# LoRA A read in place from 32 small transfers on two queues, in a conditional-LoRA and mixture-of-experts kernel

## The chip, the cores and the metric

One core of one Trainium2 chip runs the program. The metric is device time in microseconds (us) of one execution, as the median of several runs. The profiled execution is one run more, taken by the hardware profiler, with times counted from its first instruction.

## The reference

x is 32 sequences of 32 tokens of 512 numbers. Each sequence picks one of 32 adapters. The first part is a dense layer with that sequence's low-rank addition (rank 16, scaled by 2); its result feeds a router over 16 experts in 4 groups, of which each token takes two, and a shared feed-forward part.

```python
base_out = jnp.einsum('bti,oi->bto', x, W) + b
A = lora_As[adapter_mapping]              # (32, 512, 16)
Bm = lora_Bs[adapter_mapping]             # (32, 16, 512)
lora_h = jnp.einsum('bti,bir->btr', x, A)
xt = base_out + jnp.einsum('btr,bro->bto', lora_h, Bm) * SCALING
logits = xt @ router_w + router_b         # softmax, bias, two groups of four, two experts
h = silu(xt @ w1 + b1) * (xt @ w2 + b2)   # for each expert, weighted by its gate; the same once, shared
out = x + sum_e gate_e * (h_e @ w3 + b3) + shared
```

## The kernel before

The 1024 tokens are worked in two halves of 512 (`n` = 0, 1), the 512 dimensions in 4 chunks of 128 (`KC`, `k` or `m`). Products that need precision are made of three (`product`, L990): each operand is split into a rounded part (`_h`, a cast by ScalarE) and a remainder (`_l`, whole minus rounded, a subtraction by VectorE in `rest`, L680).

Every engine runs a program written out by hand, in order, and semaphores join them; a wait therefore holds everything that is written behind it on the same engine. The order around the change is this.

TensorE (from L1101) makes 10 warm-up products, then the dense layer of the first half chunk by chunk (`cond_first`), of the second half block by block (`cond_second`), and between them the LoRA work in 4 groups of 8 sequences (`g`): `turn_lora` turns the group's gathered A through PSUM bank 6, `lora_h` multiplies x by it, `cond_lora(n)` adds the low-rank part of a half. `logits_turned` and `logits` are the router, `shared_up` the shared part. Much later come `dense_up`, the two most used experts (from L1161), and the gathered rest.

GpSimd (L372) makes constants, then gathers rows of `lora` (a row is 512 numbers of A and 512 of B) by index, a group of 128 rows a transfer (`gather_lora`, L392); the last two wait for the buffer of the first two. The indices come from VectorE (L675 to L678).

SyncE (L316) only issues transfers: x's first half, six small ones, then, behind a wait for that half, the second half; behind the gather of group 1 the shared weights (`sw12`) and two more; then the stores of x's turned rows `xt_rows` for each half (L339, behind `xt_ready`), x again (L345), the two dense experts' weights (L354), and so on, all in one queue.

ScalarE (L456) issues the dense layer's weights, casts, copies A back from PSUM (`copy_loraA`), and issues the 4 MB of zeros for `y_rows` (L527), behind a wait for the last gather. Its later casts `hi_w12e` (L564) are those of the dense experts' weights. VectorE (L654) makes the remainders, masks the LoRA product (`mask_lh`), turns x's rows (`turn_xt`), chooses the experts (`choose`) and subtracts for the dense experts (`lo_w12e`).

Of the kernel before, what the change touches and what calls it, by code (L numbers as in the profile page):

```python
# [14 lines left out]
P = 128  # L15
# [6 lines left out]
SEQ_PER_GROUP = P // RANK  # L22
COLS, QUARTER = 32, P // 32
# [28 lines left out]
def program(nc, x, xT, seq_slot, condWT, cond_b, lora, router_w, router_b, router_bias,  # L52
# [5 lines left out]
    with ExitStack() as ctx:  # L58
# [30 lines left out]
        def at(kib, name, shape, dt=F32):  # L89
# [13 lines left out]
        zeros = at(16, "zeros", [P, DIM])  # L103
# [29 lines left out]
        lora_raw = at(152, "lora_raw", [P, 2, 2 * DIM])  # L133
        loraA_sb = at(160, "loraA_sb", [P, KC, P])
        lhT_split = at(162, "lhT_h", [P, 2, GT], F32R), at(164, "lhT_l", [P, 2, GT], F32R)
# [25 lines left out]

        slot_i = sb("slot_i", [P, GROUPS_L], I32)
# [50 lines left out]
        seq_in, small_in, x_in, sw3_in = (  # L213
            sem("seq_in"), sem("small_in"), sem("x_in"), sem("sw3_in"))
# [6 lines left out]
        w3_in = [sem(f"w3_in{s}") for s in range(STATIC)]  # L221
        lora_in = [sem(f"lora_in{g}") for g in range(GROUPS_L)]

        condW_hi, condW_done = sem("condW_hi"), sem("condW_done")
        xT_hi, xT_done, sw12_hi, sw12_done = sem("xT_hi"), sem("xT_done"), sem("sw12_hi"), sem("sw12_done")
        loraA_copied, xt_whole, loraB_hi, loraB_done = (
            sem("loraA_copied"), sem("xt_whole"), sem("loraB_hi"), sem("loraB_done"))
        zeros_ready = sem("zeros_ready")
# [3 lines left out]
        loraA_turned, lh_done, lh_masked = sem("loraA_turned"), sem("lh_done"), sem("lh_masked")  # L232
# [35 lines left out]
        def cond_bank(n, m):  # L268
            return bank[(4, 0, 1, 2)[m] if n else m]
# [5 lines left out]
        def unit_bank(u, m):  # L275
            return bank[((3, 6), (4, 0), (1, 2), (3, 7), (4, 0), (1, 2), (6, 1), (4, 0))[u][m]]
# [8 lines left out]
        def gate_bank(s):  # L285
            return bank[(4, 0)[s % 2]]
# [4 lines left out]
        def sum_bank(i):  # L291
            return bank[(2, 7, 6, 1, 4, 0, 3, 5)[i]]

        def turned_bank(b):
            return bank[(6, 1)[b % 2]]

        def y_bank(b):
            return bank[(2, 7)[b % 2]]
# [18 lines left out]
        def _(sp):  # L317
            def load_xT(n, k):
                sp.dma_start(xT_raw[n][:, k, :], xT[n, k]).then_inc(xT_in[n * KC + k], 16)  # L319

            load_xT(0, 0)
            sp.dma_start(slot_i[:], seq_slot).then_inc(seq_in, 16)
            for k in range(1, KC):
                load_xT(0, k)
            sp.dma_start(condb_sb[:], cond_b).then_inc(small_in, 16)
            sp.dma_start(rw_sb[:], router_w).then_inc(small_in, 16)
            sp.dma_start(rb_col[:], router_b).then_inc(small_in, 16)
# [45 lines left out]
        def _(pool):  # L373
# [18 lines left out]
            def gather_lora(g):  # L392
                if g >= 2:
                    pool.wait_ge(loraA_turned, g - 1)
                    pool.wait_ge(loraB_done, g - 1)
                pool.indirect_dma_start(lora_raw[:, g % 2, :], None, lora,
                                        bass.IndirectOffsetOnAxis(ap=lora_row[:, g:g + 1], axis=0)).then_inc(lora_in[g], 16)

            pool.wait_ge(lora_row_ready, 1)
            gather_lora(0)  # L400
            gather_lora(1)
            pool.memset(zeros[:], 0.0).then_inc(zeros_set, 1)
# [7 lines left out]
            gather_lora(2)  # L410
            gather_lora(3)


            pool.wait_ge(logits_done, BATCHES)
            pool.memset(gate[:], 0.0).then_inc(pool_step, 1)
            pool.wait_ge(pool_step, 6)
# [40 lines left out]
        def _(act):  # L457
# [10 lines left out]
            def copy_loraA(g):  # L468
                act.wait_ge(loraA_turned, g + 1)
                if g >= 1:  # L470
                    act.wait_ge(lh_done, g)
                act.copy(loraA_sb[:], bank[6][:].rearrange("p (k r) -> p k r", k=KC)).then_inc(loraA_copied, 1)  # L472

            def hi_loraB(g):
                act.wait_ge(lora_in[g], 16)
                if g >= 2:
                    act.wait_ge(cond_done, KC)
                act.copy(loraB_split[0][:, g % 2], lora_raw[:, g % 2, DIM:2 * DIM]).then_inc(loraB_hi, 1)

            def hi_lhT(g):  # L480
                act.wait_ge(lh_masked, g + 1)
                if g >= 2:
                    act.wait_ge(cond_done, KC)
                act.copy(lhT_split[0][:, g % 2], lhT_sb[:]).then_inc(lhT_hi, 1)
# [25 lines left out]
            for k in range(KC):  # L510
                hi_condW(k)
                hi_xT(0, k, k + 1)
# [8 lines left out]
            act.wait_ge(small_in, 16 * 6)  # L521
            for m in range(KC):
                whole_xtT(0, m)
                hi_xtT(0, m)
            act.wait_ge(zeros_set, 1)
            act.wait_ge(lora_in[3], 16)
# [3 lines left out]
            hi_loraB(2)  # L530
            copy_loraA(2)
            hi_sw12(0)
            hi_lhT(2)
# [33 lines left out]

            gate_silu(0)
# [11 lines left out]
            hi_w12e(1)  # L580
            act.wait_ge(sw3_in, 16)
# [27 lines left out]
            for n in range(2):  # L609
                act.wait_ge(gateT_done, n + 1)  # L610
                act.copy(gateT[:, n * 512:(n + 1) * 512], bank[(5, 6)[n]][0:STACK, :]).then_inc(gateT_copied, 1)
# [43 lines left out]
        def _(dve):  # L655
# [19 lines left out]
            dve.wait_ge(seq_in, 16)  # L675
            then(dve.tensor_copy(slot_f[:], slot_i[:]))
            then(dve.tensor_scalar(slot_f2[:], slot_f[:], float(RANK), None, ALU.mult))
            dve.tensor_scalar(lora_row[:], slot_f2[:], part16[:, 0:1], None, ALU.add).then_inc(lora_row_ready, 1)  # L678

# [8 lines left out]
            def lo_xT(n, first, last):  # L688
                hi, lo = xT_split[n]
                dve.wait_ge(xT_hi, last if n == 0 else KC + last // 2)  # L690
                rest(lo[:, first:last], xT_raw[n][:, first:last], hi[:, first:last], xT_done)

            def lo_lora(g):
                dve.wait_ge(loraB_hi, g + 1)
                rest(loraB_split[1][:, g % 2], lora_raw[:, g % 2, DIM:2 * DIM], loraB_split[0][:, g % 2], loraB_done)

            def mask_lh(g):
# [10 lines left out]
                rest(lhT_split[1][:, g % 2], lhT_sb[:], lhT_split[0][:, g % 2], lhT_done)  # L708
# [9 lines left out]
            def lo_sw12(m):  # L718
                dve.wait_ge(sw12_hi, m + 1)
                rest(sw12_split[1][:, m], sw12_raw[:, m], sw12_split[0][:, m], sw12_done)  # L720
# [30 lines left out]

            for k in range(KC):
                lo_condW(k)
                lo_xT(0, k, k + 1)
            then(dve.tensor_copy(cols[:], cols_i[:, 0:BPAD]))
# [5 lines left out]
            lo_xT(1, 0, 2)  # L761
            lo_lora(0)
            lo_xT(1, 2, 4)
            lo_lora(1)
            dve.wait_ge(consts_ready, 5)
            mask_lh(0)
            mask_lh(1)
            for m in range(KC):
                turn_xt(0, m)
                lo_xtT(0, m)  # L770
            lo_lora(2)
            lo_sw12(0)
            mask_lh(2)
            lo_lora(3)
            dve.wait_ge(small_in, 16 * 6)
            shift_logits(0)
            mask_lh(3)
# [554 lines left out]
```

## Time and profile before

| | |
|---|---|
| median of 3 runs | 132.3 us (130.42, 132.3, 249.07) |
| profiled execution | 131.28 us, span 129.5 us |
| TensorE busy | 123.5 us, 95% of the span |
| VectorE busy | 86.0 us, 66% |
| ScalarE busy | 48.3 us, 37% |
| GpSimd busy | 19.8 us, 15% |
| transfers | 28.77 MB, mean 222 GB/s |

A busy TensorE counts overlapping products, so its share says that it seldom waits, not that it works at its peak. Lines as L993 are lines of the kernel; a helper's line serves many steps. Register, branch and issuing instructions do not count as busy; a queue's own issues stand under SPq, ACTq or POOLq. A wait is put down to the event that came last.

### The profile page before, as it was taken

To read this page: it belongs to the slowest core of one execution; us is meant where nothing else is said; L and a number is where in the kernel's file an instruction comes from. 1 tells how busy PE (TensorE), PEld (TensorE's weight loads), DVE (VectorE), ACT (ScalarE), POOL (GpSimd) and SP (SyncE) were. 2 spreads that over 40 slices of the span, in tenths; PEclk is the share of its full clock that TensorE was granted. 3 is DMA by queue.
4 is the path that set the end of the run, shared out by engine and by line. 5 is a ranking of instruction groups with operands and counts; after the bars stand their busy time and mean duration, and the time that the engine had idled before them with its cause. 6 is when DMAs were issued, how large, how long until landed. Compare 5 with 4: busy or idle time off the path is not lost.

```text
span 129.5 us, 2241 instructions
## 1 busy us (share of the span) xinstructions
PE 123.5 (95%) x815; PEld 102.3 (79%) x815; DVE 86.0 (66%) x194; ACT 48.3 (37%) x85; POOL 19.8 (15%) x33
## 2 busy tenths in 40 slices
PE   6999996999996999999999999999999999999991
PEld 6988874987885777888888889987788888888891
DVE  1496095497469718989999984355906279997731
ACT  1780373595559516203963574441022110000000
POOL 7374025000000020000027200033620000000000
PEclk9999999999999999999999999999999999999999
DMA  4999888659999699989305899402426999422222
GB/s 102 375 287 347 259 331 273 225 199 370 317 301 309 140 178 175 321 305 358 123 0 116 321 309 384 161 11 83 162 86 209 328 369 375 179 97 109 110 94 81
DMA packets 16908, 28.77 MB, mean 222 GB/s; under 512 B 1952, under 2 KB 6432, under 8 KB 16768
## 3 DMA queue, kind: packets, MB, share of 16 engines
q1 hardware_dynamic: 11728, 17.07, 40.5%
q10 hardware_dynamic: 3952, 7.34, 16.5%
q0 software_dynamic: 1216, 4.20, 10.3%
q8 instruction: 7, 0.11, 0.3%
q14 instruction: 5, 0.04, 0.1%
HBM read 19.17 MB, written 9.44 MB: 221 GB/s over the span
## 4 chain that ended last, share of the span: by engine, by line
PE 77%; DMA 9%; DVE 5%; ACT 3%; issue 2%; SPq 2%; DVEq 0%; ACTq 0%
PE bank L993 58%; DMA xT_raw<-in_xT 9%; PE bank L1192 6%; PE bank L1206 3%; PE bank L1049 2%; ACT xT_h L462 2%; PE bank L1267 1%; PE bank L1060 1%; PE bank L1037 1%; PE bank L1182 1%; SPq L319 1%; DVE sw_l L682 1%; ACT loraA_sb L472 1%; PE bank L1023 1%; PE bank L1097 1%
## 5 line engine op out<-in xcount | busy, mean ns | idle before, releaser
L993 PE MATMUL bank<-xtT_h,sw_h 128*128 128x512 f32 x32 | 12.9, 405 | 1.2 <-DVE sw_l L682 1.2
L993 PE MATMUL bank<-xtT_h,w12e_h 128*128 128x512 f32 x32 | 13.1, 409 | 0.0
L993 PE MATMUL bank<-xtT_h,w12e_l 128*128 128x512 f32 x32 | 12.5, 391 | 0.0
L993 PE MATMUL bank<-xtT_l,w12e_h 128*128 128x512 f32 x32 | 12.5, 391 | 0.0
L993 PE MATMUL bank<-xtT_h,sw_l 128*128 128x512 f32 x32 | 12.5, 390 | 0.0
L993 PE MATMUL bank<-xtT_l,sw_h 128*128 128x512 f32 x32 | 12.5, 390 | 0.0
L966 DVE SCALAR_TENSOR_TENSOR x_sb<-rows_sb,val,x_sb 128x512 f32<-128x512 f32 x16 | 11.7, 748 | 0.2
L972 DVE TENSOR_TENSOR x_sb<-x_sb,bank 128x512 f32<-128x512 f32 (+1 forms) x9 | 5.6, 626 | 4.8 <-PE bank L993 4.8
L682 DVE TENSOR_TENSOR xT_l<-xT_raw,xT_h 128x512 fp32r<-128x512 f32 (+1 forms) x6 | 5.2, 867 | 4.5 <-ACT xT_h L462 4.5
L993 PEld LDWEIGHTS bank<-xtT_h,sw_h 128*128 128x128 f32 x32 | 6.0, 188 | 2.8 <-DVE sw_l L682 1.4
L790 DVE SCALAR_TENSOR_TENSOR heT_sb<-bank,b_dense,sg_sb 128x512 f32<-128x512 f32 x4 | 3.0, 751 | 7.7 <-PE bank L993 7.7
L1192 PEld LDWEIGHTS bank<-xgT_sb,w_ring 128*128 128x128 f32 x64 | 7.5, 192 | 0.5 <-issue 0.5
L430 POOL DMA_INDIRECT y_rows<-y_ring,slot_row x4 | 5.2, 1306 | 17.3 <-DVE y_ring L896 17.0
L1192 PE MATMUL bank<-xgT_sb,w_ring 128*128 128x128 f32 x64 | 7.8, 275 | 0.0
L426 POOL DMA_INDIRECT xg_sb<-xt_rows,slot_tok x4 | 4.2, 1058 | 19.2 <-DVE slot_tok L860 18.3
L993 PEld LDWEIGHTS bank<-xtT_h,w12e_h 128*128 128x128 f32 x32 | 6.0, 188 | 1.4 <-issue 0.2
L993 PEld LDWEIGHTS bank<-xtT_l,w12e_h 128*128 128x128 f32 x32 | 6.0, 188 | 1.4 <-issue 0.2
L993 PEld LDWEIGHTS bank<-xtT_h,w12e_l 128*128 128x128 f32 x32 | 6.0, 188 | 1.3
L993 PEld LDWEIGHTS bank<-xtT_h,sw_l 128*128 128x128 f32 x32 | 6.0, 188 | 1.3
L993 PEld LDWEIGHTS bank<-xtT_l,sw_h 128*128 128x128 f32 x32 | 6.0, 188 | 1.1
L462 ACT CAST xT_h<-xT_raw 128x512 fp32r<-128x512 f32 (+1 forms) x6 | 4.6, 762 | 6.1 <-DMA xT_raw<-in_xT 6.1
L993 PE MATMUL bank<-xT_h,condW_h 128*128 128x512 f32 x16 | 6.8, 423 | 0.0
(184 smaller groups left out, 294.1 us busy)
## 6 DMA issues: line engine op xcount, KB each, us to landing
y_rows<-zeros ACTq DMA_DIRECT2D x2, 2048.0 KB, 12.2
rows_sb<-y_rows SPq DMA_DIRECT2D x8, 512.0 KB, 8.4
xT_raw<-in_xT SPq DMA_DIRECT2D x8, 256.0 KB, 5.8
xt_rows<-xt_turned SPq DMA_DIRECT2D x8, 256.0 KB, 8.1
x_sb<-in_x SPq DMA_DIRECT2D x1, 2048.0 KB, 11.2
w_ring<-in_w_turned SPq DMA_DIRECT2D x4, 512.0 KB, 9.0
out<-x_sb ACTq DMA_DIRECT2D x7, 256.0 KB, 2.0
condW_raw<-in_condWT ACTq DMA_DIRECT2D x4, 256.0 KB, 4.5
```

Of the source, the lines that this page charges most:

```text
L319: sp.dma_start(xT_raw[n][:, k, :], xT[n, k]).then_inc(xT_in[n * KC + k], 16)
L426: pool.indirect_dma_start(xg_sb[:, s, :], None, xt_rows, bass.IndirectOffsetOnAxis(ap=slot_tok[:, b:b + 1], axis=0)).then_inc(landed, 16)
L430: pool.indirect_dma_start(y_rows, bass.IndirectOffsetOnAxis(ap=slot_row[:, b:b + 1], axis=0), y_ring[:, s, :], None).then_inc(landed, 16)
L462: act.copy(xT_split[n][0][:, first:last], xT_raw[n][:, first:last]).then_inc(xT_hi, 1)
L682: dve.tensor_tensor(lo, whole, hi.bitcast(F32), ALU.subtract).then_inc(made_sem, 1)
L790: dve.scalar_tensor_tensor(out=unit_part(hid_sb, u), in0=unit_bank(u, 1)[:], scalar=bias, in1=sg_sb[:, u % 2, :], op0=ALU.add, op1=ALU.mul ...
L966: add(i, dve.scalar_tensor_tensor(out=sums(i), in0=rows_sb[:, k, i, :], scalar=val[:, k, i:i + 1], in1=sums(i), op0=ALU.mult, op1=ALU.add))
L972: dve.tensor_tensor(sums(i)[:, where], sums(i)[:, where], sum_bank(0 if half else i)[:, where], ALU.add).then_inc(acc_done, 1)
L993: mm = pe.matmul(out, a[p], b[q], start=(start and n == 0), stop=(stop and n == 2))
L1049: mm = pe.matmul(cond_bank(n, m)[:, at:at + GT], loraB_split[q][:, g % 2, m * P:(m + 1) * P], lhT_split[p][:, g % 2, :], start=False, stop ...
L1192: mm = pe.matmul(half[:, 0:P], w12_ring[:, ring, (2 * k + m) * INTER:(2 * k + m + 1) * INTER], xgT[:, k, :], start=(k == 0), stop=(k == KC ...
L1206: pe.matmul(y_bank(b)[:], hT_sb[:, b % 2, :], w3_ring[:, b, :], start=True, stop=True).then_inc(y_done, 1)
```

## The change

A is laid out as (slot, 128 partitions, 16 ranks, 4 chunks), so that a sequence's A lands in place as 256 bytes in each partition and needs no turning. In each group four sequences come by SyncE (a register load of the slot, then a transfer at that offset) and four by GpSimd (an indirect gather each, with indices that GpSimd works out itself). B is gathered alone, 4 transfers. Buffers for B and the LoRA rows hold all four groups, zeros and A have other places, and the PSUM banks are dealt out anew. The first chunk of x is cast by VectorE in place of ScalarE.

```diff
 SyncE
+            def load_loraA(g):
+                for s in range(g * SEQ_PER_GROUP, g * SEQ_PER_GROUP + BY_REGISTER):
+                    slot = sp.value_load(seqs_sb[0:1, s:s + 1], min_val=0, max_val=SLOTS - 1)
+                    sp.dma_start(loraA_sb[:, s * RANK:(s + 1) * RANK, :], lora_A[bass.ds(slot, 1)].rearrange("s p r k -> p (s r) k")
+                                 ).then_inc(loraA_in[g], 16)
             load_xT(0, 0)
-            sp.dma_start(slot_i[:], seq_slot).then_inc(seq_in, 16)
+            sp.dma_start(seqs_sb[:], seqs.partition_broadcast(P)).then_inc(seqs_in, 16)
             for k in range(1, KC):
                 load_xT(0, k)
...
+            sp.dma_start(slot_i[:], seq_slot).then_inc(seq_in, 16)
+            for k in range(KC):
+                load_xT(1, k)
+            sp.wait_ge(seqs_in, 16)
+            load_loraA(0)
+            load_loraA(1)
+            sp.dma_start(sw12_raw[:], sw12).then_inc(sw12_in, 16)
...
+            load_loraA(2)
+            load_loraA(3)
...
-            sp.wait_ge(xT_in[KC - 1], 16)
-            for k in range(KC):
-                load_xT(1, k)
-            sp.wait_ge(lora_in[1], 16)
-            sp.dma_start(sw12_raw[:], sw12).then_inc(sw12_in, 16)
 GpSimd
+            pool.memset(zeros[:], 0.0).then_inc(zeros_set, 1)
+            pool.wait_ge(seqs_in, 16)
...
+            def gather_loraA(g):
+                for s in range(g * SEQ_PER_GROUP + BY_REGISTER, (g + 1) * SEQ_PER_GROUP):
+                    pool.indirect_dma_start(loraA_sb[:, s * RANK:(s + 1) * RANK, :].rearrange("p r k -> p (r k)"), None, lora_A_rows,
+                                            bass.IndirectOffsetOnAxis(ap=loraA_row[:, s:s + 1], axis=0)
+                                            ).then_inc(loraA_gathered[g], 16)
...
+            gather_loraA(0)
             pool.wait_ge(lora_row_ready, 1)
-            gather_lora(0)
-            gather_lora(1)
+            gather_loraB(0)
+            gather_loraA(1)
+            gather_loraB(1)
+            gather_loraA(2)
+            gather_loraA(3)
+            gather_loraB(2)
+            gather_loraB(3)
...
+            pool.wait_ge(sw12_hi, 2)
+            pool.tensor_tensor(sw12_split[1][:, 1], sw12_raw[:, 1], sw12_split[0][:, 1].bitcast(F32), ALU.subtract
+                               ).then_inc(sw12_done[1], 1)
 ScalarE
             hi_xT(1, 0, 2)
+            hi_xT(1, 2, 4)
             hi_loraB(0)
-            copy_loraA(0)
-            hi_xT(1, 2, 4)
+            hi_lhT(0)
             hi_loraB(1)
-            hi_lhT(0)
-            copy_loraA(1)
             hi_lhT(1)
+            hi_sw12(0)
...
+            hi_lhT(2)
+            hi_loraB(2)
             act.wait_ge(zeros_set, 1)
-            act.wait_ge(lora_in[3], 16)
             for k in range(K):
                 act.dma_start(y_rows[k * T:(k + 1) * T, :].rearrange("(i p) d -> p i d", p=P),
...
+            hi_sw12(1)
+            copy_lgT(0)
+            hi_lhT(3)
             hi_loraB(3)
-            copy_lgT(0)
-            copy_loraA(3)
             exps(0)
-            hi_lhT(3)
-            hi_sw12(1)
 VectorE
+            dve.wait_ge(xT_in[0], 16)
+            dve.tensor_copy(xT_split[0][0][:, 0, :], xT_raw[0][:, 0, :]).then_inc(first_hi, 1)
...
             for m in range(KC):
-                turn_xt(0, m)
                 lo_xtT(0, m)
-            lo_lora(2)
-            lo_sw12(0)
             mask_lh(2)
+            lo_lora(2)
+            mask_lh(3)
             lo_lora(3)
-            dve.wait_ge(small_in, 16 * 6)
+            dve.wait_ge(small_in, 16 * 3)
             shift_logits(0)
-            mask_lh(3)
+            turn_xt(0, 0)
             choose(0)
-            lo_sw12(1)
+            for m in range(1, KC):
+                turn_xt(0, m)
             dve.wait_ge(lgT_done, 1)
+            dve.wait_ge(xt_ready, KC)
             for m in range(KC):
                 turn_xt(1, m)
 TensorE
             def lora_h(g):
-                pe.wait_ge(loraA_copied, g + 1)
+                pe.wait_ge(loraA_in[g], 16 * BY_REGISTER)
+                pe.wait_ge(loraA_gathered[g], 16 * (SEQ_PER_GROUP - BY_REGISTER))
...
-            cond_first(0)
-            cond_first(1)
-            cond_first(2)
-            pe.wait_ge(consts_ready, 4)
-            turn_lora(0)
-            cond_first(3)
+            for k in range(KC):
+                cond_first(k)
             lora_h(0)
-            turn_lora(1)
-            cond_second(0, 0, KC // 2)
+            cond_second(0, 0, KC)
             lora_h(1)
-            cond_second(0, KC // 2, KC)
+            cond_second(1, 0, KC)
             cond_lora(0)
-            cond_second(1, 0, KC)
-            turn_lora(2)
             cond_second(2, 0, KC)
             lora_h(2)
             logits_turned(0)
-            turn_lora(3)
+            lora_h(3)
             cond_second(3, 0, KC // 2)
+            pe.wait_ge(consts_ready, 4)
             logits(0)
-            lora_h(3)
             cond_second(3, KC // 2, KC)
             cond_lora(1)
-            pe.wait_ge(sw12_done, 2)
+            pe.wait_ge(sw12_done[0], 1)
             shared_up(0, (0,))
             logits_turned(1)
+            pe.wait_ge(sw12_done[1], 1)
             shared_up(0, (1,), 0, KC // 2)
```

On ScalarE the cast of the shared part's third weight (L582) also waits for the zeros to have landed, since they now lie in its place.

## Rows read from the trace of the kernel before

**Rows 1.** Waits of TensorE, whole run (engine line waited for: us, times, longest)

```profile
PE bank L993 <- DVE sw_l L682: 1.2, 1, 1.2
...
PE bank L1037 <- ACT loraA_sb L472: 1.1, 1, 1.1
```

**Rows 2.** Chain of waits in order of time (start us, us, what)

```profile
23.44 2.86 PE bank L1049 x24
26.30 2.75 PE bank L993 x12
29.05 0.44 PE bank L1023 x4
...
36.52 0.44 DVE lhT_sb L703
...
37.84 0.14 DVE red L733
...
40.77 1.23 DVE sw_l L682
...
63.95 8.29 PE bank L993 x36
```

**Rows 3.** Timeline of TensorE and ScalarE to 18 us (start, us, engine, line, op)

```profile
1.13 4.63 PE L1103 MATMUL bank<-lhT_sb 128*128 128x128 f32 x20 [1.13 <-DVE lhT_sb L671]
...
4.97 0.61 ACT L462 CAST xT_h<-xT_raw 128x512 fp32r<-128x512 f32 x1
...
17.49 0.65 PE L1037 MATMUL bank<-xT_raw,loraA_sb 128*32 128x64 f32 x32
```

**Rows 4.** Timeline of GpSimd, two gathers

```profile
7.33 1.39 POOL L396 DMA_INDIRECT lora_raw<-in_lora,lora_row  x1 [0.31 <-issue]
...
69.99 0.95 POOL L426 DMA_INDIRECT xg_sb<-xt_rows,slot_tok  x1 [0.30 <-issue]
```

**Rows 5.** Issues of transfers (KB each, median us from issue to landing)

```profile
lora_raw<-in_lora,lora_row POOLq DMA_INDIRECT x4, 5.9
...
y_rows<-y_ring,slot_row POOLq DMA_INDIRECT x4, 3.2
...
x_sb<-in_x SPq DMA_DIRECT2D x1, 2048.0 KB, 11.2
```

**Rows 6.** Timeline of SyncE's issues, 70 to 72 us

```profile
70.16 0.33 SPq L349 DMA_DIRECT2D w_ring<-in_w  x1
...
71.25 0.33 SPq L349 DMA_DIRECT2D w_ring<-in_w_turned  x1
```

**Rows 7.** Tile zeros: its instructions (duration ns), and its two transfers to landing

```profile
L528 ACTq DMA_DIRECT2D y_rows<-zeros x2: 392/500/608, 26.4 to 26.8; - x2
...
DMA to landing us min/median/max: 7.7/12.2/16.6
```

**Rows 8.** Timeline of SyncE's issues, 29 to 48 us

```profile
29.29 8.17 SPq L343 DMA_DIRECT2D xt_rows<-xt_turned  x4
...
44.41 3.41 SPq L343 DMA_DIRECT2D xt_rows<-xt_turned  x4
...
47.86 1.43 SPq L345 DMA_DIRECT2D x_sb<-in_x  x1
```

**Rows 9.** Timeline of VectorE, four turnings of x's rows

```profile
41.90 2.48 DVE L716 STREAM_TRANSPOSE xt_turned<-xtT_whole 128x512 f32<-128x512 f32 x4
```

**Rows 10.** Timeline of ScalarE, first cast of the dense weights

```profile
61.59 1.05 ACT L566 CAST w12e_h<-w12e_raw 128x1024 fp32r<-128x1024 f32 x1
```

**Rows 11.** Stretches: busy by engine, then PEclk, DMA share, GB/s

```profile
28.00:30.00 2.00, 2.00 (x12) 1.69 (x11) 2.00 (x5) 1.96 (x4) 0.00 (x0) 1.00 1.04 360
...
44.00:46.00 2.00, 2.00 (x38) 1.37 (x36) 0.38 (x1) 0.00 (x0) 0.00 (x0) 1.00 0.55 113
...
46.00:48.00 2.00, 2.00 (x13) 1.65 (x10) 0.14 (x1) 0.37 (x1) 0.18 (x1) 1.00 0.99 172
...
129.00:129.50 0.50, 0.00 (x0) 0.00 (x0) 0.00 (x0) 0.00 (x0) 0.00 (x0) 0.50 0.00 0
```

More of the change, by code:

```diff
@@ L22 @@
 SEQ_PER_GROUP = P // RANK
+BY_REGISTER = SEQ_PER_GROUP // 2
 COLS, QUARTER = 32, P // 32
@@ L102, in program @@
         w12e_raw = at(8, "w12e_raw", [P, DENSE, W12])
-        zeros = at(16, "zeros", [P, DIM])
+        loraA_sb = at(16, "loraA_sb", [P, SEQS * RANK, KC])
+        zeros = at(148, "zeros", [P, DIM])
         w3e_raw = at(16, "w3e_raw", [P, DENSE, DIM])
@@ L221, in program @@
         w3_in = [sem(f"w3_in{s}") for s in range(STATIC)]
+        loraA_in = [sem(f"loraA_in{g}") for g in range(GROUPS_L)]
+        loraA_gathered = [sem(f"loraA_gathered{g}") for g in range(GROUPS_L)]
         lora_in = [sem(f"lora_in{g}") for g in range(GROUPS_L)]
         condW_hi, condW_done = sem("condW_hi"), sem("condW_done")
[L225 to L228, printed above, removed]
+        xT_hi, xT_done, sw12_hi = sem("xT_hi"), sem("xT_done"), sem("sw12_hi")
+        sw12_done = [sem(f"sw12_done{m}") for m in range(2)]
+        xt_whole, loraB_hi, loraB_done = sem("xt_whole"), sem("loraB_hi"), sem("loraB_done")
+        first_hi, zeros_ready = sem("first_hi"), sem("zeros_ready")
         lhT_hi, lhT_done, xtT_hi, xtT_done = sem("lhT_hi"), sem("lhT_done"), sem("xtT_hi"), sem("xtT_done")
@@ L268, in cond_bank @@
         def cond_bank(n, m):
-            return bank[(4, 0, 1, 2)[m] if n else m]
+            return bank[(4, 6, 0, 1)[m] if n else m]
         def unit_of(u):
@@ L610, in _ @@
                 act.wait_ge(gateT_done, n + 1)
-                act.copy(gateT[:, n * 512:(n + 1) * 512], bank[(5, 6)[n]][0:STACK, :]).then_inc(gateT_copied, 1)
+                act.copy(gateT[:, n * 512:(n + 1) * 512], bank[(5, 2)[n]][0:STACK, :]).then_inc(gateT_copied, 1)
             act.wait_ge(w3e_in, 16 * DENSE)
@@ L689, in lo_xT @@
                 hi, lo = xT_split[n]
-                dve.wait_ge(xT_hi, last if n == 0 else KC + last // 2)
+                if n == 0 and first == 0:
+                    dve.wait_ge(first_hi, 1)
+                else:
+                    dve.wait_ge(xT_hi, first if n == 0 else KC - 1 + last // 2)
                 rest(lo[:, first:last], xT_raw[n][:, first:last], hi[:, first:last], xT_done)
@@ L754, in _ @@
                 lo_xT(0, k, k + 1)
+                if k == 1:
+                    dve.wait_ge(seq_in, 16)
+                    then(dve.tensor_copy(slot_f[:], slot_i[:]))
+                    then(dve.tensor_scalar(slot_f2[:], slot_f[:], float(RANK), None, ALU.mult))
+                    dve.tensor_scalar(lora_row[:], slot_f2[:], part16[:, 0:1], None, ALU.add).then_inc(lora_row_ready, 1)
             then(dve.tensor_copy(cols[:], cols_i[:, 0:BPAD]))
@@ L1004, in cond_first @@
                 pe.wait_ge(condW_hi, k + 1)
-                pe.wait_ge(xT_hi, k + 1)
+                if k == 0:
+                    pe.wait_ge(first_hi, 1)
+                else:
+                    pe.wait_ge(xT_hi, k)
                 over_dims(w_hi, x_hi, k == 0)
@@ L1012, in cond_second @@
             def cond_second(m, first, last):
-                if m >= 1 and first == 0:
-                    pe.wait_ge(xtT_hi, m)
+                if m >= 2 and first == 0:
+                    pe.wait_ge(xtT_hi, m - 1)
                 for k in range(first, last):
@@ L1049, in cond_lora @@
                             mm = pe.matmul(cond_bank(n, m)[:, at:at + GT], loraB_split[q][:, g % 2, m * P:(m + 1) * P],
-                                           lhT_split[p][:, g % 2, :], start=False, stop=(p == 1 and g % 2 == 1))
+                                           lhT_split[p][:, g, :], start=False, stop=(p == 1 and g % 2 == 1))
                     mm.then_inc(cond_done, 1)
```

126 lines of the change are left out of this document (60 added, 66 removed).

## The prediction

> **What bounds it now.** I read the page first, then the waits of TensorE, then the chain of waits in order of time, then the stretch up to 67 us engine by engine. TensorE is the bound nearly everywhere: its own waits come to three, of which two lie in the changed stage: 1.1 us for a turned LoRA A and 1.2 us for a remainder of the shared weights [rows 1]. The chain shows what else the old order puts on TensorE: four turnings of A, of 0.44 us where it shows one alone, then the products [rows 2]. From the end of that remainder, 40.77 + 1.23 = 42.0 [rows 2], TensorE runs without a gap to the end. So removing A's turnings and both waits offers about 4 x 0.44 + 2.3 = 4.1 us at most, and a step is worth its time only if what replaces it is ready at TensorE's pace.
>
> **First x cast by VectorE: at most 0.1 us.** ScalarE's first cast of x ends at 4.97 + 0.61 = 5.58, but the warm-up products hold TensorE until 1.13 + 4.63 = 5.76 [rows 3]. VectorE's cast moves only what is hidden there. I take 0.
>
> **Turning A dropped.** The first LoRA product starts at 17.49 [rows 3]. Without one turning and the wait of about 0.2 before it, it starts at 16.9, if A is there. A strided weight load is not shown in any row; between 0 and a doubling of the 0.65 us of one LoRA product [rows 3] I take 0, because those loads overlap, and keep 4 x 0.65 = 2.6 us for the upper end.
>
> **GpSimd's queue.** In place of 4 gathers there are 20, in the order A0 (4), B0, A1 (4), B1, A2 (4), A3 (4), B2, B3. One gather held GpSimd 1.39 us while VectorE ran subtractions with two inputs, and 0.95 us in a quieter stretch, with 0.3 of issue before each [rows 4]: 1.25 to 1.7 us a gather. About 14 of the 29 us in which they run hold such subtractions, so I take 1.4. [...]
>
> The indices need four small steps on GpSimd behind the sequence list, which lands at about 4.7; first gather at 6.0. Number n (from 0) starts at 6.0 + 1.4 n. Landing: a 256 KB scatter took 3.2 us, a 512 KB gather in a full queue 5.9 [rows 5]; I take 3.3 for 32 KB of A and 4.0 for 256 KB of B, nearer the first because the queues are then nearly empty; both ends stay. So A1 is in at 20.5, B1 at 22.6, A3 at 33.1, B2 at 35.2, B3 at 36.6. [...]
>
> **SyncE's queue.** A register load and a transfer behind it take 71.25 - 70.16 = 1.09 us [rows 6]. Eight of them from about 5.6 end at 14.4, where the shared weights are issued, hardly another time than now; the other eight end at 25. GpSimd, not SyncE, is the later half of each group. x's second half is issued at 3.7 instead of 8.85, behind the first half in the same queue, and no longer holds anything.
>
> **TensorE up to the shared product.** Second half, first block 16.9 + 0.6 + 2.75 = 20.25; LoRA product 1 waits for A1 until 20.5, ends 21.1; next block 23.9. The LoRA sum then waits for B1: cast 0.62, subtraction 0.69, then mask, cast and subtraction of the LoRA rows (0.44, 0.41, 0.42 as the first such row has it) make 25.3 [rows 2]; it ends at 27.9, where the old order stood at 26.30 with one block of 2.75 less [rows 2]. Next block 30.65; LoRA product 2 and router product 32.1; product 3 waits for A3: 33.1 to 33.75; half a block to 35.15. Here it meets a **new wait**: the router's copy stands on ScalarE behind B2's cast, the two issues of zeros (0.39 + 0.61) and the cast of 1.05: 35.2 + 0.62 + 1.0 + 1.05 + 0.36 = 38.25. Then 0.1, half a block 1.4 and the sum 2.86 [rows 2]: 42.6, against 42.0. What was saved is given back: +0.6 us. The subtraction sent to GpSimd (1.23 on VectorE [rows 2]; slower there at most by some us) is wanted only after 45 and costs nothing.
>
> **The queue of transfers behind it, the larger term.** Two orders move much later. The 4 MB of zeros are issued by ScalarE behind B2's cast: 35.85 instead of about 26.40 (both issues, 26.4 to 26.8 [rows 7]). The turning of x's rows, first half, goes behind the choice of experts: B3's cast ends at 39.3, its subtraction 40.0, shift 0.5, one turn 0.62, choice 3.0 (37.84 to 40.77 [rows 2]), three turns [rows 9]: 46.0, where the stores stood at 29.29 [rows 8]. SyncE's order is stores of both halves, x again (2 MB), then the dense expert's weights, one queue. Now: zeros and first half take 26.40 to 26.8 + 16.6 = 43.4, 17.0 us [rows 7]; second half and x from 44.41 to 47.86 + 11.2 = 59.1, 14.65 us [rows 5, 8]; the first dense weights are in by 61.59, 2.5 later [rows 10]. Less 0.9 for the half-empty stretch at 44 to 46 (share 0.55 [rows 11]) this is 33.25 us of work: 35.85 + 33.25 = 69.1. Cast 1.05 [rows 10] and subtraction 1.22 follow: the dense product can start at 71.5. TensorE reached it at 63.95 + 2.75 = 66.7 [rows 2] and would at 67.3. So the end moves by 71.5 - 66.7 = **+4.8 us**. The lower bound: zeros all hidden, stores at the 172 GB/s of [rows 11] (2.1 MB in 12.2 us from 46.0), the remaining 2.6 MB at 360 GB/s: 65.5, +1.2 us. I take the sum, since it was measured on the same transfers.
>
> The profiled run took 131.28 us (span 129.5 and 1.8 around it); the runs shown have 130.42 and 132.3 beside one of 249, so the median of 132.3 is 1 above it. 131.28 + 4.8 = **136.1 us**.
>
> **Rivals.**
> 1. *Gathers at 1.25 us throughout.* For it: 0.95 + 0.30 [rows 4]; against: the 1.39 beside subtractions. B2 is in 2.7 earlier, TensorE's own path ends at 39.9, 2.1 us ahead of before: 129.2 us, faster. It decides if the dense weights land by about 62.2; zeros and rows 2.7 earlier give 62.8 by the lower bound, 66.4 by the sum (133.4).
> 2. *Gathers at 1.7 and a lowered clock.* B2 lands at 40.6, the weights at 74.5: 141.5 us. [...]
> 3. *A is not copied in whole rows:* the register transfers leave the last dimension of 4 numbers unmerged, so 256 bytes go as 16-byte pieces, 2048 each. The stores of 512 rows already held SyncE 8.17 us for four [rows 8]; four times as many pieces in 16 transfers would cost tens of us. Little speaks for it, as rows that are contiguous on both sides merge elsewhere.
>
> **Chances.** Within 2% is within 2.6 us, about what a measurement tells apart. Forecast 0.42 (its own range 132.5 to 139; 0.06 of it within 2%), quick gathers 0.34 (0.10 faster by over 2%, if A's stores also drain early; 0.24 within), slow gathers or clock 0.20, broken rows 0.04. Faster 0.10, same 0.30, slower 0.60. The range leaves out a tenth on each side: 130.0 to 140.5.
>
> **What would show it.** GpSimd's gathers 1.4 us apart and B2's cast near 35; the zeros issued near 36; TensorE idle before the router's transposition (some 3 us) and before the first dense product, the latter ended by VectorE's subtraction of the dense weights, behind their transfer; row stores near 46. I am wrong if the dense weights land before 64, if gathers come closer than 1.25 us, or if TensorE waits for SyncE's half of A instead.

## The result, and the profile after

The changed kernel took 141.21 us (median of 4 runs, 140.44 to 141.53). Beside it the kernel before took 131.5 (median of 4, 130.42 to 249.07; the longest is a disturbed run and no part of the ratio). The ratio is 1.076, with a 95% interval of 1.064 to 1.088: slower. The forecast was 136.1 us with a range of 130.0 to 140.5, so the sign and the place of the loss came and the size did not. The profiled run took 141.53 us, span 139.8, against a span of 129.5 before: 10.3 us to explain.

The page after: busy time by engine, TensorE's and the clock's line over 40 slices of 3.5 us, and the chain that ended last.

```profile
PE 125.2 (90%) x799; PEld 102.7 (73%) x799; DVE 87.7 (63%) x194; ACT 46.2 (33%) x80; POOL 39.4 (28%) x54
...
PE   6949992999978999999905999999999999999992
...
PEclk9999999599999999999985699999999999999999
...
PE 45%; SPq 8%; DMA 7%; DVE 3%; ACT 1%; issue 1%; ACTq 0%
PE bank L1031 33%; DMA w12e_raw<-in_w 7%; SPq L360 6%; PE bank L1222 5%; PE bank L1236 2%; PE bank L1297 1%; PE bank L1212 1%; SPq L369 1%; SPq L362 1%; DVE w12e_l L708 1%; DVE xt_turned L745 1%; ACT w12e_h L595 1%; PE bank L1133 1%; PE bank L1197 1%; DVE hsT_sb L828 1%
```

Two large holes stand in TensorE's line, in the slices from 21 and from 70 us, and behind each the clock is lower. In the chain the transfers come in: the dense weights' transfer and SyncE's row stores, neither of which was there before. The waits of TensorE name the holes (engine, line, waited for: us, times, longest); they answer to [rows 1].

```profile
PE bank L1031 <- DVE hsT_sb L828: 5.2, 1, 5.2
PE bank L1073 <- issue: 2.7, 1, 2.7
PE bank L1040 <- ACT xT_h L499: 1.8, 1, 1.8
...
PE bank L1085 <- DVE loraB_l L708: 1.1, 1, 1.1
PE bank L1102 <- ACT lgT L530: 0.2, 1, 0.2
```

The 5.2 us is the first dense product. The chain in order of time (start us, us, what; 52 pieces from 40 to 80 us) shows what it waited for, and answers to [rows 2].

```profile
46.91 1.20 DVE xt_turned L745 x2
...
60.58 9.82 DMA w12e_raw<-in_w
...
70.50 1.05 ACT w12e_h L595
...
71.57 1.23 DVE w12e_l L708
72.80 0.35 DVE ncmp L890
...
73.17 0.43 DVE val L891
...
73.62 0.30 DVE sc L892
...
73.95 0.76 DVE hsT_sb L828
...
74.85 5.30 PE bank L1031 x13
```

VectorE turns x's rows, SyncE issues eight stores of them and x, and the dense weights, issued at 60.58, land 9.82 us later behind all that; the zeros are not in this chain. Then come the cast, the subtraction, and what the forecast had not priced: VectorE's next four instructions, the last of them the hidden layer of the shared part (L828), on which TensorE also waits. The dense product starts at 74.85; before, it started at 63.95 + 2.75 = 66.7 [rows 2]. That is 8.15 us.

The stretches (us, busy by engine, then granted clock, DMA share, GB/s) give the rest.

```profile
4.00:6.00 2.00, 2.00 (x14) 1.76 (x13) 1.49 (x3) 0.62 (x1) 0.00 (x0) 1.00 0.36 103
...
26.00:28.00 2.00, 2.00 (x6) 1.60 (x5) 1.01 (x3) 1.35 (x2) 1.70 (x2) 0.50 0.20 45
...
74.00:76.00 2.00, 1.15 (x3) 0.99 (x4) 1.90 (x6) 2.00 (x4) 0.49 (x1) 0.50 0.00 0
76.00:78.00 2.00, 2.00 (x7) 1.52 (x6) 1.79 (x8) 0.63 (x2) 1.70 (x2) 0.50 0.21 37
78.00:80.00 2.00, 2.00 (x8) 1.58 (x7) 1.86 (x7) 0.67 (x2) 1.39 (x3) 0.67 0.84 176
```

After the hole TensorE runs at a granted clock of 0.50 until about 79. The lost work, estimated from these rows, is 1.15 x 0.5 + 2.0 x 0.5 + 2.0 x 0.33 = 2.2 us. 8.15 + 2.2 = 10.35: this is the whole difference of the spans. The same happens in small behind the 2.7 us wait, at 26 to 28, where the clock is 0.50 too.

GpSimd's timeline answers to [rows 4]; VectorE's and ScalarE's behind it show what ran beside it (start us, us, engine, line, operation, in brackets the idle time before).

```profile
6.84 0.21 POOL L411 CAST seqs_f<-seqs_sb 128x32 f32<-128x32 int32 x1 [2.87 <-DMA seqs_sb<-in_seqs]
...
8.37 1.69 POOL L423 DMA_INDIRECT loraA_sb<-in_lora_A,loraA_row  x1 [0.30 <-POOL loraA_row L416]
10.37 0.95 POOL L423 DMA_INDIRECT loraA_sb<-in_lora_A,loraA_row  x1 [0.30 <-issue]
...
32.56 0.95 POOL L428 DMA_INDIRECT lora_raw<-in_lora_B,lora_row  x1 [0.30 <-issue]
...
39.02 2.40 POOL L449 TENSOR_TENSOR sw_l<-sw_raw,sw_h 128x1024 fp32r<-128x1024 f32 x1 [2.31 <-ACT sw_h L526]
```

```profile
37.17 0.42 DVE L708 TENSOR_TENSOR lhT_l<-lhT_sb,lhT_h 128x256 fp32r<-128x256 f32 x1 [0.48 <-ACT lhT_h L513]
...
39.53 2.17 DVE L708 TENSOR_TENSOR lhT_l<-lhT_sb,lhT_h 128x256 fp32r<-128x256 f32 x1 [0.82 <-ACT lhT_h L513]
```

```profile
36.81 0.39 ACTq L562 DMA_DIRECT2D y_rows<-zeros  x1
```

The first gather starts at 8.37, not 6.0, and most of the 20 then follow 1.25 us apart, not 1.4. Four took longer (1.01 to 1.69 us), which makes 1.34 on average; B2's is issued at 32.56. SyncE's issues answer to [rows 6, 8].

```profile
7.88 8.00 SPq L331 DMA_DIRECT2D loraA_sb<-in_lora_A  x8
18.53 8.51 SPq L331 DMA_DIRECT2D loraA_sb<-in_lora_A  x8
...
48.12 9.10 SPq L360 DMA_DIRECT2D xt_rows<-xt_turned  x8
57.26 1.40 SPq L362 DMA_DIRECT2D x_sb<-in_x  x1
60.58 1.36 SPq L366 DMA_DIRECT2D w12e_raw<-in_w  x2
```

A register load and its transfer take 8.00 / 8 = 1.0 us on SyncE, near the 1.09 of the forecast. The stores start at 48.12 where they started at 29.29 [rows 8].

### The profile page after: what moved, and what is told of

Its sections match the earlier page's. It is cut to its first block, busy times and chain, and to the rows that moved or that the text cites. A ratio compares the mean times of both kernels' runs of the same rounds, so it can differ in the third digit from the quotient of the medians.

```text
span 139.8 us, 2317 instructions
## 1 busy us (share of the span) xinstructions
PE 125.2 (90%) x799; PEld 102.7 (73%) x799; DVE 87.7 (63%) x194; ACT 46.2 (33%) x80; POOL 39.4 (28%) x54
## 2 busy tenths in 40 slices
DMA packets 19611, 28.77 MB, mean 206 GB/s; under 512 B 4656, under 2 KB 9136, under 8 KB 19472
## 4 chain that ended last, share of the span: by engine, by line
PE 45%; SPq 8%; DMA 7%; DVE 3%; ACT 1%; issue 1%; ACTq 0%
PE bank L1031 33%; DMA w12e_raw<-in_w 7%; SPq L360 6%; PE bank L1222 5%; PE bank L1236 2%; PE bank L1297 1%; PE bank L1212 1%; SPq L369 1%; SPq L362 1%; DVE w12e_l L708 1%; DVE xt_turned L745 1%; ACT w12e_h L595 1%; PE bank L1133 1%; PE bank L1197 1%; DVE hsT_sb L828 1%
## 5 line engine op out<-in xcount | busy, mean ns | idle before, releaser
L1031 PE MATMUL bank<-xtT_h,w12e_h 128*128 128x512 f32 x32 | 14.2, 443 | 5.2 <-DVE hsT_sb L828 5.2
L423 POOL DMA_INDIRECT loraA_sb<-in_lora_A,loraA_row x16 | 16.8, 1051 | 4.9 <-issue 4.6
L1031 PE MATMUL bank<-xtT_l,w12e_h 128*128 128x512 f32 x32 | 13.3, 414 | 0.0
L1031 PE MATMUL bank<-xtT_h,w12e_l 128*128 128x512 f32 x32 | 13.2, 413 | 0.0
L1031 PEld LDWEIGHTS bank<-xtT_h,w12e_h 128*128 128x128 f32 x32 | 6.5, 204 | 7.1 <-issue 5.8
L708 DVE TENSOR_TENSOR xtT_l<-xtT_whole,xtT_h 128x512 fp32r<-128x512 f32 x8 | 5.6, 737 | 4.3 <-ACT xtT_h L521 4.3
L828 DVE SCALAR_TENSOR_TENSOR heT_sb<-bank,b_dense,sg_sb 128x512 f32<-128x512 f32 x4 | 3.0, 750 | 7.7 <-PE bank L1031 7.6
L1031 PEld LDWEIGHTS bank<-xtT_l,w12e_h 128*128 128x128 f32 x32 | 6.6, 206 | 1.6 <-issue 0.2
L1031 PEld LDWEIGHTS bank<-xtT_h,w12e_l 128*128 128x128 f32 x32 | 6.5, 202 | 1.5
L1031 PE MATMUL bank<-xT_h,condW_h 128*128 128x512 f32 x16 | 7.3, 455 | 0.0
```

Of the source, the lines that this page charges most:

```text
L423: pool.indirect_dma_start(loraA_sb[:, s * RANK:(s + 1) * RANK, :].rearrange("p r k -> p (r k)"), None, lora_A_rows, bass.IndirectOffsetOnA ...
L708: dve.tensor_tensor(lo, whole, hi.bitcast(F32), ALU.subtract).then_inc(made_sem, 1)
L828: dve.scalar_tensor_tensor(out=unit_part(hid_sb, u), in0=unit_bank(u, 1)[:], scalar=bias, in1=sg_sb[:, u % 2, :], op0=ALU.add, op1=ALU.mul ...
L1031: mm = pe.matmul(out, a[p], b[q], start=(start and n == 0), stop=(stop and n == 2))
```

## The experiments

The theory, from the two traces: most of the loss has nothing to do with how A is read. **The queue:** zeros (issued by ScalarE) and the stores of x's turned rows (by SyncE) were moved behind the LoRA work, the dense weights come behind the stores and x in SyncE's queue, and VectorE's order and the clock add to the wait. The rival: **the LoRA stage**, late at its start and paced by the gathers, pulls everything behind it late.

### 1. The dense weights ahead of x

```diff
 SyncE, changed kernel
-            sp.wait_ge(cond_done, HALVES_T * KC)
-            sp.dma_start(x_sb[:], ...)
             ...
             for j in range(DENSE):
                 load_one(w12e_raw[:, j, :], w12, dense[j], w12e_in[j])
+            sp.wait_ge(cond_done, HALVES_T * KC)
+            sp.dma_start(x_sb[:], ...)
```

> Changed kernel, with the dense experts' weights issued ahead of x in SyncE's queue. Queue theory (the 10 us come from the dense weights landing at 70.4 behind the row stores and x; VectorE then stands in order before its hidden product, TensorE waits 5.2 us and its clock falls): the weights land near 63, TensorE's wait of 5.2 us is gone, dense products start near 69.7 and at the full clock: 141.2 - 5.2 - 2.3 = 133.7 us. Rival, late LoRA (the gathers put TensorE behind and that sets the end): 141 us, unchanged. Rival, clock alone: below 141 by 2.3 at most.

Measured: 134.1 us, ratio to before 1.027 (1.022 to 1.032), some 7 us off the changed kernel with two transfers moved past one. Its waits of TensorE:

```profile
PE bank L1073 <- issue: 2.5, 1, 2.5
PE bank L1102 <- ACT lgT L530: 1.3, 1, 1.3
...
PE bank L1085 <- DVE loraB_l L708: 1.1, 1, 1.1
PE bank L1040 <- ACT xT_h L499: 1.0, 1, 1.0
PE bank L1073 <- DMA loraA_sb<-in_lora_A,loraA_row: 0.8, 1, 0.8
```

The wait of 5.2 is gone, and so is the lowered clock (1.00 from 68 to 76). What is left, 2.7%, arises ahead of the shared product, which starts at 44.8 in place of 42.04: the waits above all lie before it, most of them in the LoRA stage.

### 2. The late queue without the LoRA change

```diff
 kernel before: ScalarE, then VectorE
-            act.wait_ge(zeros_set, 1); act.wait_ge(lora_in[3], 16); two issues of zeros
             ...
             hi_lhT(3)
             hi_sw12(1)
+            act.wait_ge(zeros_set, 1); two issues of zeros
-                turn_xt(0, m)
                 lo_xtT(0, m)
             ...
             choose(0)
             lo_sw12(1)
+            for m in range(KC):
+                turn_xt(0, m)
+            dve.wait_ge(xt_ready, KC)
```

> Kernel before, with A still turned, but the zeros issued behind the second cast of the shared weights (near 38 in place of 26.4) and x's first rows turned behind the choice of experts (stores near 44.5 in place of 29.3). Queue theory: the late stores alone bring the loss: dense weights land near 68.5, dense products start near 72.8 in place of 66.7, clock 2.3: about 139.6 us against 131.3. Rival, late LoRA: no more than 132 us, as A is as before.

Measured: 140.69 us, ratio 1.073 (1.065 to 1.081). The wait of TensorE, then SyncE's issues:

```profile
PE bank L994 <- DVE hsT_sb L791: 6.9, 1, 6.9
```

```profile
43.80 12.53 SPq L343 DMA_DIRECT2D xt_rows<-xt_turned  x8
56.37 1.99 SPq L345 DMA_DIRECT2D x_sb<-in_x  x1
59.92 1.11 SPq L349 DMA_DIRECT2D w12e_raw<-in_w  x2
```

With A gathered and turned as before, two moved steps alone bring a loss of the same size. This is the strongest run for the queue: it has none of the small gathers, no register transfer and no list in it. TensorE comes to the dense product some 3.5 us earlier than in the changed kernel and waits longer there, so what the LoRA stage costs is hidden behind that wait.

### 3. The hidden layer ahead of the subtraction

```diff
 VectorE, changed kernel
+            hidden(1)
             lo_w12e(0)
             ...
-            hidden(1)
```

> Changed kernel, with VectorE's hidden(1) ahead of the subtraction of the dense weights. Queue theory with the order on VectorE as a term of its own: the dense products start when the subtraction ends, 72.8 in place of 74.85: 139.2 us, and down to 137 if the shorter idleness spares the clock. Rival, only the landing counts and what stands behind it on VectorE does not: 141 us.

Measured: 138.88 us (137.31 to 140.42), ratio 1.062 (1.055 to 1.069). The wait is then put down to the subtraction itself:

```profile
PE bank L1030 <- DVE w12e_l L708: 3.3, 1, 3.3
```

So hidden(1) stood in the way, and nothing but its place behind the subtraction held it. The four runs spread over 3 us, and in the profiled one, the fastest, the clock did not fall (mean 0.998; the other three have 0.963 to 0.988); the 2.3 us can't be parted cleanly into order and clock.

### 4. TensorE kept busy through the wait

```diff
 TensorE, changed kernel, ahead of the first dense product
+            for _ in range(24):
+                pe.matmul(bank[2][:], sw12_split[0][:, 0, 0, 0:P], xtT_split[0][0][:, 0, :], start=True, stop=True)
             pe.wait_ge(w12e_done, 1)
```

The 24 products are read by nobody.

> Changed kernel, with 24 further products of 512 columns into a free PSUM bank ahead of TensorE's wait for the dense weights (about 5.5 us of work in the wait of 5.2; their result is not used). Clock as a term of its own: the granted clock stays at 1.00 past 73 us, the 24 products behind the wait take 5.5 us in place of 7.8, the wait itself stays: 141.2 - 2.3 = 138.9 us, a little more where the added products outlast the wait. Rival, the clock costs nothing because something else is as late: 141 us.

Measured: 139.25 us, ratio 1.061 (1.057 to 1.066), 2.0 us less than without them, though the weights came no earlier (cast at 71.16). One stretch of it, which answers to that of the changed kernel:

```profile
76.00:78.00 2.00, 2.00 (x10) 1.63 (x10) 1.81 (x5) 1.18 (x3) 1.52 (x2) 1.00 0.00 0
```

The clock's share of the loss is about 2 us, shown by filling the idleness and changing nothing else. The two profiled runs agree: here the dense product starts 0.7 us later (75.57 against 74.85) and the span is 1.4 us shorter.

### 5. The list laid out 128 times

```diff
-            sp.dma_start(seqs_sb[:], seqs.partition_broadcast(P))
+            sp.dma_start(seqs_sb[:], seqs)
-        "seqs": np.asarray(itok_B_0_23).reshape(SEQS),
+        "seqs": np.tile(np.asarray(itok_B_0_23).reshape(1, SEQS), (P, 1)),
```

> Changed kernel, with the list of sequences laid out 128 times in memory instead of read 128 times from one place. Theory of the stalled start (the 128 reads of one line hold all transfer queues from 4 to 6 us, where the share is 0.36): that stretch fills to about 1, the second chunk's weights land 2 us earlier, TensorE's wait of 1.8 us near 9 is gone, gathers start near 6.3 in place of 8.4, all behind moves by about 2: 139.2 us. Rival, x's early second half is what delays the weights: stretch and time unchanged, 141 us.

Measured: 140.85 us, ratio 1.077 (1.072 to 1.081): the time hardly moves, a miss. The stretch shows that the cause of the stalled start was right all the same:

```profile
4.00:6.00 2.00, 2.00 (x13) 1.75 (x12) 1.47 (x3) 1.22 (x2) 1.29 (x4) 1.00 0.98 289
```

Transfers run at 289 GB/s in place of 103 (before: 392 in the same stretch), TensorE no longer waits for x, and the first gather starts at 7.33. But a TensorE that starts earlier waits longer for A of group 1, 3.5 us in place of 2.7, and the dense weights are cast only 1.1 us earlier (69.4). What is saved at the start is mostly spent at the next gates.

### 6 to 8. Zeros early, turnings early, both

```diff
 ScalarE (6, 8): the zeros behind the casts of x's second half, in place of behind B2's cast
             hi_xT(1, 2, 4)
+            act.wait_ge(zeros_set, 1); two issues of zeros
 VectorE (7, 8): x's first half turned as before
             for m in range(KC):
+                turn_xt(0, m)
                 lo_xtT(0, m)
```

Zeros early:

> Changed kernel, with the zeros issued behind the cast of x's second half, near 15 us in place of 36.8; row stores as changed. Queue theory: the stores start at 48 as before and fill the queue from there by themselves, so the dense weights land 1 us earlier at most: 140 us, within 139 to 141.5. Rival, the zeros' lateness is the loss: dense weights near 62 and 134 us.

Turnings early:

> Changed kernel, with x's first rows turned as before, each ahead of its subtraction (first stores near 37 in place of 48); zeros as changed, near 37. Queue theory: work of 30 to 33 us still begins at 37, dense weights land at 67 to 70: 138 to 141 us. Rival, the late turn is the loss: dense weights near 62 and 134 us.

Both:

> Changed kernel, with both: zeros near 15 us and x's first rows turned early. Queue theory: zeros are gone by 30, first stores by 46, the dense weights land near 62 and TensorE's wait of 5.2 us and the lower clock go, as with the dense weights ahead of x: 134 us, up to 136 if zeros delay the gathers. Rival, late LoRA: 141 us.

Measured: 144.88 us (ratio 1.104, 1.095 to 1.112), 139.9 (1.067, 1.057 to 1.077) and 137.65 (1.050, 1.045 to 1.054). The zeros alone were the worst miss, both together one of 2 to 4 us; only the turnings came as expected. The run with early zeros: the gathers' issue (median us to landing), the waits of TensorE, and two issues of SyncE.

```profile
loraA_sb<-in_lora_A,loraA_row POOLq DMA_INDIRECT x16, 8.5
```

```profile
PE bank L1073 <- DMA loraA_sb<-in_lora_A,loraA_row: 6.3, 1, 6.3
PE bank L1031 <- DVE hsT_sb L828: 4.4, 1, 4.4
```

```profile
52.22 8.77 SPq L360 DMA_DIRECT2D xt_rows<-xt_turned  x8
...
64.18 1.08 SPq L366 DMA_DIRECT2D w12e_raw<-in_w  x2
```

Small gathers that landed in 3.8 us took 8.5 beside 4 MB of zeros, and the queues, full from 16 to 32 (314 to 388 GB/s), then stood empty from 40 to 52 (2 GB/s), because the row stores had not been made yet. With both early the dense wait is gone, as the theory says, but the price is paid in the LoRA stage (6.1 us for A, clock 0.50 from 26 to 32). So early zeros are no free repair: beside them the small gathers land more than 4 us later.

Which of the two steps holds the dense weights can be read from these traces. With the zeros early they were cast at 73.80, 21.6 us behind the first store; in the changed kernel it is 70.50, 22.4 us behind it. So in the changed kernel too the landing goes by the stores and x, and the zeros, in by 37.23 + 13.9 = 51.1 (issue and landing), count for little. With the turnings early and the zeros late, on the other hand, the weights are cast at 69.1, only 1.4 us earlier. Each step alone makes them about as late as both, which is why taking back one of them repairs little.

### 9. One part alone: the split wait, in the kernel before

```diff
 TensorE, kernel before
-            pe.wait_ge(sw12_done, 2)
+            pe.wait_ge(sw12_done, 1)
             shared_up(0, (0,))
             logits_turned(1)
+            pe.wait_ge(sw12_done, 2)
             shared_up(0, (1,), 0, KC // 2)
```

> The kernel before with one edit of the change alone: TensorE waits for the first remainder of the shared weights before the first shared product and for the second only before the second one, 2.86 us later. In the trace of before the wait there is 1.2 us and nothing else stands between. Both theories (the dense weights late in the queue; the LoRA stage slower) say nothing against it: TensorE's path to the end is 1.2 us shorter, 130.3 against 131.5 for before, ratio 0.991. If the dense weights (cast at 61.59, needed at about 65.5) or the choice of experts become the next thing late, the ratio is 1.00.

Measured: 130.03 us against 130.78, ratio 0.993 (0.990 to 0.996). It is the only version ahead of both kernels, by 0.7%. Of the 1.2 us a part comes back before the first dense product:

```profile
PE bank L993 <- DVE hsT_sb L790: 0.6, 1, 0.6
```

VectorE's hidden(1) is the next thing late, the same instruction as in run 3.

### 10. The dense weights ahead of x, in the kernel before

The edit of run 1, on the kernel before.

> The kernel before with the dense weights issued ahead of x on SyncE, the same edit that gained 7 us on the changed kernel. Queue theory: in before the weights are in 4 to 5 us before TensorE comes to them, so moving them further ahead gives nothing: ratio 1.00 (0.995 to 1.005). If the edit were a gain of its own, whatever the order around it, this would be several us faster too (ratio near 0.95).

Measured: 131.1 us against 130.78, ratio 1.004 (1.001 to 1.007). An edit worth 7 us in one kernel is worth nothing in the other, where the weights were in time.

### 11 and 12. The LoRA stage in another order

```diff
 on run 1 with the list of run 5
 GpSimd
-            gather_loraB(0)
             gather_loraA(1)
+            gather_loraB(0)
 ScalarE
+            hi_lhT(0)
             hi_loraB(0)
-            hi_lhT(0)
+            hi_lhT(1)
             hi_loraB(1)
-            hi_lhT(1)
...
             hi_lhT(2)
+            copy_lgT(0)
+            hi_lhT(3)
             hi_loraB(2)
...
+            hi_loraB(3)
             hi_sw12(1)
-            copy_lgT(0)
-            hi_lhT(3)
-            hi_loraB(3)
 VectorE
+            mask_lh(0)
             lo_lora(0)
-            mask_lh(0)
+            mask_lh(1)
             lo_lora(1)
-            mask_lh(1)
...
             mask_lh(2)
+            for m in range(KC):        # run 12 only, in place of around choose(0)
+                turn_xt(0, m)
+            mask_lh(3)
             lo_lora(2)
-            mask_lh(3)
 TensorE (cond_lora: groups outside, blocks inside)
-            lora_h(1)
             cond_second(1, 0, KC)
+            lora_h(1)
             cond_lora(0)
```

> The changed kernel with the dense weights ahead of x, the list of sequences laid out 128 times, and the LoRA stage in another order: GpSimd gathers A of groups 0 and 1 ahead of B, TensorE makes the second block of the second half before the LoRA product 1 and the LoRA sums group by group, VectorE masks ahead of B's remainders, ScalarE copies the router's logits ahead of B's third cast and casts the second half of the shared weights last. With the dense weights first the run took 134.1 us and its trace had waits of 2.5 and 0.8 us for A, 1.3 for the logits, 1.1 for B, 1.0 for x: 6.7 in all. Theory that these waits are the whole price of reading A in place: 134.1 - 6.7 = 127.4 if all go, 129 if a third comes back elsewhere, ratio 0.98, faster than before. Rival: the small transfers slow the whole stage (start, landings), and the waits come back behind other transfers: 132 to 134, ratio 1.00 to 1.02.

> The kernel of the run before (dense weights first, list laid out 128 times, LoRA stage in another order) with the four turnings of x's first half on VectorE ahead of the mask of the last LoRA product, where VectorE waited, in place of around the choice of experts. In that run's trace TensorE came to the shared product some 2 us ahead of before and then lost 2.0 us waiting for the second choice of experts, which stood behind seven turnings of 4.48 us. Theory: the price of the change lay in the order around it, and with three turnings (1.9 us) fewer ahead of the choice the wait goes: 131.0 - 2.0 = 129.0, ratio 0.985 (0.98 to 0.99), faster than before. Rival: the turnings delay the mask and with it the LoRA product 3 or the remainders of x's first half, and the time comes back: 130.5 to 131.5, ratio 1.00.

Measured: run 11 130.96 us, ratio 1.001 (0.999 to 1.003); run 12 132.37, ratio 1.013 (1.008 to 1.017). Run 11 lies between the two theories: 3.1 us of the 6.7 came off. Its profiled execution took 133.31, above its median; its rows stand for the order of events only. The shared product starts there at 40.7, against 42.04 before, but TensorE then waits 2.0 us for the second choice of experts, behind this on VectorE:

```profile
44.07 4.48 DVE L745 STREAM_TRANSPOSE xt_turned<-xtT_whole 128x512 f32<-128x512 f32 x7
```

In run 12 that wait is gone and the rival came true: the turnings hold the mask (36.19 in place of 34.89), and TensorE waits in the sum of the second half.

```profile
PE bank L1084 <- DVE loraB_l L708: 2.4, 3, 1.1
```

So most of the price of reading A in place is an order that it unsettles. With the dense weights first, the list laid out and this order the kernel ties with before; no order tried here makes it faster.

One piece of the change was left in place in every run: the subtraction sent to GpSimd. In run 11 it ran beside VectorE's first steps of the choice:

```profile
39.25 2.42 POOL L449 TENSOR_TENSOR sw_l<-sw_raw,sw_h 128x1024 fp32r<-128x1024 f32 x1 [3.20 <-ACT sw_h L526]
```

```profile
40.30 1.45 DVE L764 TENSOR_TENSOR tmp<-ex,red 128x64 f32<-128x64 f32 x1
```

The same small product takes 0.22 us in the changed kernel (at 43.66) and 1.62 in run 12, and each time that it is long it ends 0.1 us behind GpSimd's. Estimated from these rows, 1.2 of the 2.0 us of run 11's wait for the second choice come from there; no run moves the subtraction back to VectorE.

## Why the prediction was half right

**Right:** the sign; that SyncE would not bind (1.0 us a register transfer against 1.09 taken); that the first x cast, the turnings' removal and the wait before the shared product would not show in the end; and the place of the loss, the dense weights behind zeros, row stores and x. Rivals 1 and 3 fell: 16 of the 20 gathers did come at 1.25, but the weights were late anyway, and A landed as whole rows (19611 packets in the whole run, where 16 transfers of 2048 pieces would make 32768). Rival 2's price of 141.5 lies beside the measured 141.2 by luck: it rests on gathers 1.7 us apart, and the mean was 1.34. The working has two slips that moved nothing much: 25.3 + 2.86 is 28.2, not 27.9, which the wait for A3 absorbs, and 69.1 + 1.05 + 1.22 is 71.4, not 71.5.

**Wrong, term by term:**

1. *"I take 1.4" and "first gather at 6.0".* Both were off, and the second gives back less than half of the first: 2.4 us later at the start, 1.34 us a gather on average. B2's gather was issued at 32.56, where the forecast has 6.0 + 18 x 1.4 = 31.2; the zeros went out at 36.81 in place of 35.85. The forecast took two-input subtractions on VectorE to lengthen half the gathers. The four that took 1.01 us or more (at 8.37, 12.87, 25.43 and 28.33) all began while one ran; the other 16 took 0.94 to 0.95, also where a subtraction began during the gather (as at 11.62 and 15.44), and even two that began while one ran (at 16.69 and 27.09). The late start is the list: 128 copies of one 128-byte line, whose stretch ran at 103 GB/s (run 5).
2. *Dense weights in at 69.1.* They were in by 70.40. The forecast adds up an unbroken queue from the zeros on, and by that sum the zeros' delay would be 0.96 of the 1.3 us. But the landing goes by the stores and x (runs 6 to 8), and the stores, forecast at 46.0, were seen at 48.12. That the sum came so near is in part luck: the zeros had drained 3 us after the stores began.
3. *"Cast 1.05 and subtraction 1.22 follow: the dense product can start at 71.5."* **This step failed.** TensorE waits for two things there, and the second, hidden(1), stands on VectorE behind the subtraction: 72.80 to 74.85, 2.05 us. The changed kernel's code had it in plain sight, in an order that before hardly made felt: there hidden(1) ended at 66.26, 0.4 us ahead of the first dense product. Run 3 moved it and the wait fell to 3.3.
4. *The clock.* It stood among the rivals and in the chances ("slow gathers or clock 0.20"), and the sum put it at nothing. The wait came to 5.2 us, the granted clock behind it was 0.50 until about 79, and that cost 2.0 us (run 4). It belonged in the sum, because the forecast's own main term was the wait behind which it fell.
5. *TensorE's path to the shared product, +0.6.* It starts at 45.0 (the row below: that product's duration in ns, shortest, median and longest, first and last start), 3.0 later than before. The first product starts 0.8 earlier (4.96), where the forecast took 0.1 at most, but then TensorE waited 1.8 for x, 2.7 for A1 (0.25 forecast) and 1.1 for B3, and the clock was low at 24 to 28 (0.68, then 0.50); of the waits forecast for B1, A3 and the router's copy only 0.2 came. A's gathers landed in 3.0 to 5.4 us, median 3.8, where the forecast took 3.3. Behind the dense wait this cost nothing; with the wait gone it is the 2.7% of run 1.

```profile
L1031 PE MATMUL bank<-xtT_h,sw_h x32: 389/389/501, 45.0 to 68.8; 128*128 128x512 f32 x32
```

The sum mended: 4.8 forecast, 1.3 for the later landing, 2.05 for hidden(1), 2.2 for the clock: 10.35 against the 10.3 between the spans.

One more term the forecast put at nothing, because its result is wanted late: the subtraction sent to GpSimd, 2.40 us at 39.02. VectorE's lhT_l, 0.42 us at 37.17, took 2.17 at 39.53 and ended 0.28 behind GpSimd's 39.02 + 2.40. B3's remainder stood behind it (41.63 to 42.31), and TensorE came to it at 41.39: the 1.1 us wait for B3, which run 1 still has, is by an estimate from these rows the price of that subtraction, and with lhT_l at 0.42 it would be gone.

## What to carry to other kernels

When a stage is rebuilt, list what was moved out of its way, and follow each moved transfer down its queue to the next thing that stands behind it: two moved steps cost 7.3% here with the rebuilt stage left out (run 2). Where a wait is forecast, look at every semaphore that the waiting engine needs there, and at what each of their makers does first; and where the forecast's main term is a wait of TensorE, put the clock behind it into the sum, with a chance, since it did not fall after every long wait here. When work is sent to another engine, ask what it holds up there, and not only when its result is wanted. When a wait goes away, the gain is only as long as the distance to the next gate (runs 5, 9, 11, 12).

## What the runs showed of the hardware

- One 16 KB transfer that reads the same 128 bytes 128 times lowered all transfers to 103 GB/s for 2 us and landed in 5.5 us; laid out in memory it landed in 3.2 to 3.5 (runs 5, 11, 12), and the same stretch ran at 289 GB/s (run 5). In the changed kernel it was the second transfer that SyncE issued.
- GpSimd's subtraction of 128x1024 took 2.40 us, where VectorE takes 1.23 [rows 2]. Beside it VectorE's subtraction of 128x256 took 2.17 us in place of 0.42 (changed kernel), and its product of 128x64 took 1.45 and 1.62 in place of 0.22 (runs 11, 12).
- A gather of 32 KB in 128 pieces landed in 3.8 us in the changed kernel (198 GB/s from 8 to 34) and in 8.5 beside 4 MB of zeros (run 6, 362 GB/s from 15 to 32); SyncE's plain transfers of the same size landed in 2.8 in both of these runs, but in 6.8 in run 8, which has the zeros early as well. In the changed kernel the 1 MB of shared weights landed in 5.6 us, 32 times the bytes in twice the 2.8.
- The granted clock fell to 0.50 after TensorE's waits of 2.7 us (at 24 to 28) and 5.2 us (at 72 to 79) in the changed kernel, but not after 2.5 us in run 1 and 2.6 us in run 4 (1.00 from 24 to 28 in both; up to there run 4 is the changed kernel's own program) nor after 3.3 us in the profiled execution of run 3, and it did behind one of 1.9 in run 7 (0.55 at 24 to 26). What decides between them stays open.
